# Attention over 40 fields per sample on one Trainium2 core: x and y laid out in DRAM in eight runs of rows per transfer, with a gap behind each run

## What is computed

```
q = x Wq^T + bq     k = x Wk^T + bk     v = x Wv^T + bv       (each 40 x 128, as 4 heads of 32)
att[h] = softmax(q[h] k[h]^T / 8)                             (40 x 40 per head)
y = relu(concat_h(att[h] v[h]) + x Wr^T + br)                 (40 x 128)
```

## Time and profile before

| what | before |
|---|---|
| median of 3 runs | 927.33 us (925.72 to 928.43) |
| the profiled execution's own time | 923.84 us |
| its span, first to last instruction | 921.1 us |
| granted TensorE clock, mean | 0.996 |
| TensorE busy | 892.3 us (97%) |
| GpSimd busy | 872.1 us (95%) |
| ScalarE busy | 770.6 us (84%) |
| VectorE busy | 726.7 us (79%) |
| mean DMA traffic | 110 GB/s |

### The profile page before, as it was taken

The page is one execution under the profiler, slowest core; times in us unless marked ns, Lnnn a source line. Parts: engine busy times, 40 slices in busy tenths (PEclk is TensorE's granted clock), DMA queues, the critical chain, the costliest instruction groups (busy, mean ns, idle before and its releaser), DMA issues.

```text
span 921.1 us, 67888 instructions
## 1 busy us (share of the span) xinstructions
PE 892.3 (97%) x30208; PEld 626.7 (68%) x30208; DVE 726.7 (79%) x2066; ACT 770.6 (84%) x1541; POOL 872.1 (95%) x1028
## 2 busy tenths in 40 slices
PE   6999999999999999999999999999999999999996
PEld 4667666767666776676666667666667766767664
DVE  5878777878787877888887878787878887878785
ACT  4888888888888888888888888888888888888886
POOL 3999999999999999999999999999999999999997
PEclk9999999999999999999999999999999999999998
DMA  4333333333333333333333333333333333333321
GB/s 120 97 110 117 113 105 110 115 107 112 118 112 107 116 111 111 111 117 109 115 112 105 110 111 111 112 112 112 117 111 112 112 120 108 115 110 112 111 83 67
DMA packets 67429, 101.20 MB, mean 110 GB/s; under 512 B 13632, under 2 KB 46656, under 8 KB 67136
## 3 DMA queue, kind: packets, MB, share of 16 engines
q1 hardware_dynamic: 66704, 96.72, 34.7%
q10 hardware_dynamic: 432, 0.15, 0.1%
HBM read 54.88 MB, written 41.94 MB: 105 GB/s over the span
## 4 chain that ended last, share of the span: by engine, by line
PE 93%; POOL 3%; issue 2%; DVE 1%; DMA 0%; ACT 0%; POOLq 0%; ACTq 0%
PE vr_bank L422 24%; PE o_bank L475 22%; PE s_buf L406 19%; PE o_bank L386 15%; PE s_buf L452 7%; PE vr_bank L433 6%; POOL y_sum L191 1%; POOL m_diag L183 1%; POOL q_bd L199 1%; PE o_bank L390 0%; DMA biases<-bias_in 0%; ACT y_rows L238 0%; POOLq L39 0%; DVE s_buf L325 0%; PE vr_bank L438 0%
## 5 line engine op out<-in xcount | busy, mean ns | idle before, releaser
L183 POOL TENSOR_TENSOR m_diag<-m_split,ident 128x640 bf16<-128x640 bf16 x256 | 323.1, 1262 | 32.2 <-DVE m_split L336 30.1
L191 POOL TENSOR_TENSOR y_sum<-rv,y_att 128x512 f32<-128x512 f32 x256 | 303.9, 1187 | 1.9 <-DVE y_att L347 1.9
L199 POOL TENSOR_SCALAR q_bd<-q_flat,consts 128x320 f32<-128x320 f32 x512 | 267.6, 537 | 11.2 <-DVE kT L320 11.1
L422 PE MATMUL vr_bank<-w_cols,xT 64*128 64x128 f32 (+1 forms) x3072 | 269.0, 308 | 0.1
L258 ACT ACTIVATE rv<-vr_bank 128x1024 f32<-128x1024 f32 x256 | 260.4, 1017 | 0.1
L325 DVE TRANSPOSE_TENSOR_REDUCE s_buf<-s_buf 128x20 f32<-128x640 f32 x256 | 221.6, 866 | 47.8 <-PE s_buf L406 47.7
L475 PE MATMUL o_bank<-rv,pT 64*40 64x33 f32 x16384 | 229.6, 202 | 12.1 <-issue 8.4
L406 PEld LDWEIGHTS s_buf<-q_bd,kT 64*40 64x40 f32 x8192 | 151.5, 113 | 116.2 <-issue 115.1
L475 PEld LDWEIGHTS o_bank<-rv,pT 64*40 64x40 f32 x16384 | 192.9, 117 | 54.4 <-issue 17.9
L320 DVE TENSOR_SCALAR kT<-o_bank,biases 128x320 f32<-128x320 f32 x256 | 140.9, 550 | 89.1 <-PE o_bank L390 89.0
L406 PE MATMUL s_buf<-q_bd,kT 64*40 64x80 f32 x8192 | 200.5, 233 | 1.4 <-issue 1.1
(11 more groups left out here) (31 smaller groups left out, 466.0 us busy)
## 6 DMA issues: line engine op xcount, KB each, us to landing
xT<-xT_in SPq DMA_DIRECT2D x512, 104.0 KB, 2.7
y<-y_rows SPq DMA_DIRECT2D x512, 80.0 KB
w_cols<-w_in SPq DMA_DIRECT2D x1, 192.0 KB, 2.6
vr_bias<-vr_bias_in ACTq DMA_DIRECT2D x1, 128.0 KB, 3.3
consts<-consts_in ACTq DMA_DIRECT2D x1, 20.0 KB, 2.4
biases<-bias_in ACTq DMA_DIRECT2D x1, 1.0 KB, 3.8
```

The costliest lines, as they stand in the source:

```text
L183: pool.tensor_tensor(m_diag[:], m_split[:, place % 2].unsqueeze(2).to_broadcast([P, BLOCKS, QUAD]), ident[:].unsqueeze(1).to_broadcast([P, ...
L191: pool.tensor_tensor(y_sum[:, n % 3].rearrange("r (a d) -> r a d", d=DIM), rv[:, place % 4, RESIDUAL * HEADS:(RESIDUAL + SLOTS) * HEADS, 0 ...
L199: pool.tensor_scalar(q_bd[:, place % 4, :, s], q_flat[:, place % 2].rearrange("d (b f) -> d b f", f=FIELDS), consts[:, C_HEAD + s:C_HEAD + ...
L422: return nc.tensor.matmul(blocks(half, first, step)[:, 0:count], xT[rows, place % 8, PAIR * pair:PAIR * pair + P], w_cols[rows, 1:1 + coun ...
```

## The change

The two DRAM tensors get a new layout, and the two transfers address it with a pattern of three dimensions. The 64 rows of a load become 8 runs of 8 rows, the 40 rows of a store 8 runs of 5 rows; behind each run lie 16 float32 (64 bytes) that are not used. The tiles in SBUF, the rows' lengths, the bytes moved, the order of the issues and all waits are as before.

```diff
+RUNS, GAP = 8, 16
...
+            def runs(transfer, columns):
+
+                run = transfer.ap[0]
+                rows = (run[0] - GAP) // columns
+                return bass.AP(transfer.tensor, transfer.offset, [[run[0], RUNS], [columns, rows], [1, columns]])
+
             def load(n, place, lane):
-                sp.dma_start(xT[lane:lane + HALF, place % 8, 0:PAD], xT_in[n, lane:lane + HALF]).then_inc(x_loaded[place % 8], 16)
+                sp.dma_start(xT[lane:lane + HALF, place % 8, 0:PAD], runs(xT_in[n, lane // HALF], PAD)).then_inc(x_loaded[place % 8], 16)
...
-                sp.dma_start(out[n, g], y_rows[HALF * g:HALF * g + FIELDS, place % 4]).then_inc(y_stored[place % 4], 16)
+                sp.dma_start(runs(out[n, g], SLOTS * OUT), y_rows[HALF * g:HALF * g + FIELDS, place % 4]).then_inc(y_stored[place % 4], 16)
...
-        "xT_in": xT.reshape(steps, P, PAD),
+        "xT_in": np.pad(xT.reshape(steps, 2, RUNS, HALF // RUNS * PAD), ((0, 0), (0, 0), (0, 0), (0, GAP))),
...
-    args.append(nc.dram_tensor("y", (steps, 2, FIELDS, SLOTS * OUT), _mybir.dt.float32, kind="ExternalOutput").ap())
+    args.append(nc.dram_tensor("y", (steps, 2, RUNS, FIELDS // RUNS * SLOTS * OUT + GAP), _mybir.dt.float32, kind="ExternalOutput").ap())
...
-    rows = r.results[0]["y"].reshape(steps, 2, FIELDS, SLOTS, OUT)
+    rows = r.results[0]["y"][..., :-GAP].reshape(steps, 2, FIELDS, SLOTS, OUT)
```

## The result

| | before | after |
|---|---|---|
| median | 926.53 us (4 runs) | 946.36 us (942.39 to 949.66, 4 runs) |
| profiled execution, its span | 923.84, 921.1 us | 947.85, 946.1 us |
| TensorE busy | 892.3 us | 904.2 us |
| GpSimd busy | 872.1 us | 875.7 us |

A fourth run of the kernel before (922.76 us) moves its median from 927.33 to 926.53. The ratio is 1.0217, 95% interval 1.0163 to 1.0271: slower by 19.8 us. That it is slower is clear; whether by more than 2% the interval leaves open. The forecast of no change, with a range up to 934 us, missed.

What follows compares the result with a forecast made beforehand. TensorE and GpSimd were taken to set the pace, with transfers beside it: 923.84 + 0.4 (start) + 0 (steady state) + 0.1 (end) = 924.3 us profiled, 927.8 against the median. No change was forecast; 8 in 10 range 925 to 934.

Steps and rivals of the forecast that it cites:

- Eight engines per transfer: Loads and stores of x and y: 8 engines each in place of 16 and 10, 61,584 packets in queue 1.
- No wait on x or y in the steady state: Wait list: no new row naming a DMA in the steady state; slack 17 us for loads, 8 us for stores.
- The start: First 10 us, through the load of biases: queueing behind first x loads adds 0.4 us, range 0 to 1.4.
- The landing of 3.1 us: Load of x on eight engines: median landing goes from 2.7 us to about 3.1 us.
- + 0 (steady state): Steady steps: slower landings and longer issues of loads and stores add 0 us to the time.
- rivals 1: DMA engines: longer packets saturate; 10% longer gives a median about 974 us, 3% more 927 to 930; chance 0.05.
- Rival 2: TensorE's instruction fetches: late beside fuller engines, or long SP issues more frequent; 3.5 to 14 us, 931 to 942; chance 0.09.
- Nothing shows TensorE short of instructions: TensorE before L475: its idle on issue, 17.9 us in all, 63 idles of 0.28 us, read as no shortage.
- the sign that the prediction named for this: Wrong if queue 8's packets get much longer than 1.13 us and TensorE idles on issue.
- I take 0.51 for all: SyncE's issues of loads and stores: 0.51 us each, four per step making 2.04 us.
- The extra 0.1 us per step is hidden there: SyncE: longer issues vanish in its wait for TensorE, about 1.2 us per step.
- Rival 4: Instruction fetches: engines without data serve them undisturbed; half of 17.9 us before L475 goes, 918 us; chance 0.04.

Runs made afterwards that it cites:

- h2: Kernel before the change, without any load of x from step 8 on and without TensorE's wait for them: ratio 0.9864 to the kernel before.
- e3: Changed kernel with its loads in eight runs with gaps (8 engines), but stores as before the change (10 engines): ratio 1.0180 to the kernel before.
- e4: Changed kernel with its stores in eight runs with gaps (8 engines), but loads as before the change (16 engines): ratio 1.0048 to the kernel before.
- g4: As e4, but the stores in ten runs of 4 rows with gaps (10 engines, three dimensions): ratio 1.0165 to the kernel before.
- f3: As e3, but from step 8 on a load brings only the first 208 of each row's 416 columns: ratio 0.9993 to the kernel before.
- e1: Changed kernel with loads in 16 runs and stores in 10 runs of 4 rows, gaps kept (16 and 10 engines): ratio 1.0187 to the kernel before.
- e2: Changed kernel with eight runs but no gap behind a run; packets and issues were those of before: ratio 0.9998 to the kernel before.

## Why the prediction was wrong

**Right.** Eight engines per transfer, to the packet. No wait on x or y in the steady state; queue 1 at 34.7%. The start: biases landed after 4.10 us, 0.28 more (0.4 forecast), and the first L440 came at 8.99 us, 0.31 later. The landing of 3.1 us stays unchecked: the trace of the changed kernel has no landing time of a load.

**The step that failed is "+ 0 (steady state)".** Loads and stores were costed by who waits for them, and their slack was real. They cost time through a third party, TensorE's instructions. I named it in rivals 1 and 2 and set it aside with "Nothing shows TensorE short of instructions: its idle on issue before L475 is 17.9 us in all". That row was the shortage itself: 62 of its 63 idles stand at a packet border, and they are not what a change of operations leaves. Counting instructions from one idle to the next would have shown it: 256 or a multiple. h2 puts what loads cost before the change at 1.4%, 12.8 us. Rival 2 had the right mechanism with a price of 3.5 to 14 us and a chance of 0.09. The late instructions alone, e3, are 1.8%, some 17 us. Of the sign that the prediction named for this, one half came, TensorE's idle on issue, and the other did not: queue 8's packets last as long as before, but begin later.

**The issues.** "I take 0.51 for all" was too low: 0.59 for a load, 0.69 for a store, 0.82 with ten engines. "The extra 0.1 us per step is hidden there" was right for SyncE's own time: the four issues of a step take 2.57 us, not 2.04, and it still waits for the product.

```profile
SPq L146 <- PE o_bank L482: 188.4, 234, 1.5
```

It was wrong for TensorE, which pauses, or whose signal is late, where a store's after-effect meets it. Alone that is 0.5% with eight engines (e4, 13 of 232 steps with the pause) and 1.7% with ten (g4, 90 steps with the pause and 44 late signals). How often the two meet depends on the place of the issues in the step.

**Rival 1** set saturation of one engine as the point. That is not what costs the time. In g2 the rows of x take 19.3% of 16 engines, which is 77% of each of four; with the stores' 12.8%, spread over ten that include these four, it would be about 98%. Even so nobody waits for a transfer in the steady state, and the kernel is faster. Its "crowded" part holds between 8 and 16 engines and for the bytes on eight (f3), and fails at four.

**Rival 4**, faster, had a chance of 0.04: "Engines that carry no data serve fetches undisturbed", half of the 17.9 us gone, 918 us. It is wrong for eight engines and fits four: in g2 that row is 10.2 us, and 0.9908 of 926.53 us is 918.

**What explains the order 4, 16, 8** best is that a fetch is hurt only by a load on its own engine. With 16 engines each fetch may meet a load, but a short one; with eight a part of them meets one twice as long, and 20 start 1.8 to 3 us late instead of 2; with four few meet one at all. That fits the late starts (0 on four, 2 and 5 in the two traces with plain transfers, 20 on eight). It was not shown: no view tells which engine carries a fetch, and on four engines those that are hit should be hit hardest, yet none of them starts 1.8 to 3 us late. Open too is what happens some 0.3 to 0.6 us after a store's issue of three dimensions, and whether the pause and the late signal are one thing.

**A version that beats both** is g2: loads in four runs with a gap, stores as before, 0.9908 (0.9885 to 0.9931) of the kernel before.

## What to carry over

A transfer that nobody waits for is not free in a long unrolled kernel: count TensorE's instructions between its idles on issue, and if they come at multiples of 256, it is waiting for instruction packets. Data transfers can make these late, as the loads do here. Then the layout in DRAM, which sets the number of engines, is a knob worth trying at several values, since it need not be monotonic (4 engines 0.991, 8 engines 1.018, 16 engines 1). Prefer patterns that merge to two dimensions for frequent stores: here a third dimension made their issue 180 to 310 ns longer, and 0.5 to 1.7% was lost, more where more steps had the end of TensorE's product 0.3 to 0.6 us behind such an issue.

## What the runs showed of the hardware that I had not expected

- TensorE's instructions arrive just in time: at a stop the engine resumes 1.3 to 1.6 us after the packet of 256 has ended, and 36 such stops (9.7 us) were in the kernel of before. At 163 of 223 borders in the middle of that run TensorE passes within 1.65 us of the packet's end.
- A store of three dimensions (40 rows, 80 KB) takes 693 ns to issue with eight engines and 822 with ten, a plain one 513; a load 593 against 476.
- In 101 of 108 steps of e1 a semaphore of TensorE came 0.14 us late when a store's issue ended 0.2 to 0.3 us before the last matmul.
- In 114 of 232 steps of the changed kernel TensorE paused for about 0.07 us at the end of the product, 0.37 to 0.40 us after a store's issue had ended; before the change in none.
- Adjacent runs count as one, so a first dimension needs a gap to survive (e2: 66,704 packets without the gap, 61,584 with it).
